# Cross attention over 25,088 context rows: six chunks mixed at a time in place of four, with V's projections and the splits of the context two chunks sooner

## The reference, cut to what matters

```
Q = LN(x) @ Wq + bq;  K = ctx @ Wk + bk;  V = ctx @ Wv + bv      # 16 heads of 32
scores = einsum('bihd,bjhd->bijh', Q, K) / sqrt(32)
attn = softmax(scores, axis=1)                                  # over the 256 queries i
out = einsum('bijh,bjhd->bihd', attn, V) @ Wo + bo
```

## Time and profile before

| | |
|---|---|
| median of 3 runs | 2655.68 us (2654.76 to 2655.82) |
| the profiled execution's own time | 2655.65 us |
| its span, first to last instruction | 2653.9 us |
| PE busy over the span | 2607.3 us (98%) |
| PE weight loads busy | 2203.0 us (83%) |
| DVE busy | 1968.5 us (74%) |
| ACT busy | 1866.0 us (70%) |
| POOL busy | 1272.1 us (48%) |
| mean granted TensorE clock | 0.993 of full speed |
| scores, first and last start | 511.9 and 2208.8 us |

### The profile page before, as it was taken

The page is one execution under the profiler, slowest core; times in us unless marked ns, Lnnn a source line. Parts: engine busy times, 40 slices in busy tenths (PEclk is TensorE's granted clock), DMA queues, the critical chain, the costliest instruction groups (busy, mean ns, idle before and its releaser), DMA issues.

```text
span 2653.9 us, 59616 instructions
## 1 busy us (share of the span) xinstructions
PE 2607.3 (98%) x21096; PEld 2203.0 (83%) x21096; DVE 1968.5 (74%) x3882; ACT 1866.0 (70%) x6834; POOL 1272.1 (48%) x2200
## 2 busy tenths in 40 slices
PE   8998999999999999999999999999999998999998
PEld 6876999888888888888888888888888885799997
DVE  8876866587778777778777778777787776655555
ACT  2213444388888888888888888888888895345553
POOL 5532111256566556566556665565665553222222
PEclk9998999999999999999999999999999999999999
DMA  9993553566666666666666666666666653545452
GB/s 385 387 399 116 193 195 151 135 171 182 159 158 163 165 167 159 165 159 158 174 166 159 158 165 161 167 161 167 158 155 175 166 126 110 192 175 190 182 191 72
DMA packets 132300, 473.33 MB, mean 178 GB/s; under 512 B 31128, under 2 KB 31256, under 8 KB 124832
## 3 DMA queue, kind: packets, MB, share of 16 engines
q1 hardware_dynamic: 122592, 452.21, 58.9%
q10 hardware_dynamic: 9408, 17.31, 1.7%
HBM read 244.47 MB, written 17.30 MB: 99 GB/s over the span
## 4 chain that ended last, share of the span: by engine, by line
PE 97%; DVE 2%; ACT 1%; issue 0%; DMA 0%; POOL 0%; SPq 0%; DVEq 0%; POOLq 0%
PE PB L592 21%; PE PB L619 15%; PE PB L627 14%; PE PB L607 14%; PE PB L695 7%; PE PB L418 7%; PE PB L710 6%; PE PB L554 6%; PE PB L567 3%; PE PB L447 1%; PE PB L478 1%; ACT EE L858 1%; PE PB L454 1%; PE PB L499 0%; DMA AR<-in_ctx 0%
## 5 line engine op out<-in xcount | busy, mean ns | idle before, releaser
L858 ACT ACTIVATE EE<-PB,small 128x256 f32<-128x256 f32 x3136 | 1445.0, 482 | 203.5 <-DVE small L1252 190.4
L1252 DVE TENSOR_REDUCE small<-PB 128x2 f32<-128x512 f32 x1568 | 1031.1, 682 | 355.5 <-PE PB L619 355.3
L858 ACT ACTIVATION_READ_ACCUMULATOR EE<-PB,small 128x1 f32 x3136 | 664.8, 212 | 0.0
L1514 POOL TENSOR_TENSOR VS<-V,small 128x128 f32<-128x128 f32 x784 | 320.5, 409 | 700.6 <-DVE small L1258 693.1
L592 PE MATMUL PB<-CTX,WKV 128*128 128x256 f32 x4704 | 624.9, 282 | 0.0
L592 PEld LDWEIGHTS PB<-CTX,WKV 128*128 128x128 f32 x4704 | 588.5, 190 | 0.1
L619 PEld LDWEIGHTS PB<-QS,STK 128*128 128x128 f32 x3136 | 469.5, 190 | 124.9 <-issue 82.3
L619 PE MATMUL PB<-QS,STK 128*128 128x256 f32 x3136 | 555.8, 289 | 7.5 <-ACT EE L858 5.4
L607 PE MATMUL PB<-WKV,CTX 128*128 128x512 f32 x1584 | 432.6, 395 | 0.8 <-DVE V L1248 0.8
L627 PE MATMUL PB<-EE,VS 128*32 128x256 f32 x6272 | 381.5, 384 | 0.0
L607 PEld LDWEIGHTS PB<-WKV,CTX 128*128 128x128 f32 x1584 | 273.1, 190 | 37.0 <-DVE V L1248 1.2
(11 more groups left out here) (202 smaller groups left out, 2545.8 us busy)
## 6 DMA issues: line engine op xcount, KB each, us to landing
STK<-KHL SPq DMA_DIRECT2D x1568, 128.0 KB, 2.5
RW<-in_l1f SPq DMA_DIRECT2D x32, 2048.0 KB, 8.0
AR<-in_ctx SPq DMA_DIRECT2D x49, 1024.0 KB, 8.5
RAW<-in_ctx SPq DMA_DIRECT2D x98, 512.0 KB, 3.7
WF<-in_l0f SPq DMA_DIRECT2D x17, 2304.0 KB, 8.8
v_scr<-RAW ACTq DMA_DIRECT2D x64, 256.0 KB, 7.5
V<-v_scr SPq DMA_DIRECT2D x64, 256.0 KB, 2.9
WA<-in_l0a SPq DMA_DIRECT2D x1, 4096.0 KB, 14.3
```

The lines of the kernel that those rows point to most:

```text
L858: m = e.activation(EE[:, b, s, :], bank(2 * (k % 2) + half, 256 * (s % 2), 256), ACT.Exp, bias=nm[:, b, s:s + 1], accum_out=su[:, b, s:s + 1])
L1252: e.tensor_reduce(nm[:, k % RING, 2 * half:2 * half + 2], bank(2 * (k % 2) + half).rearrange("p (s i) -> p s i", s=2), axis=AX.X, op=ALU.m ...
L1514: e.tensor_tensor(VS[:, b, :].rearrange("p (s d) -> p s d", s=4), V[:, t % 4, 128 * c:128 * c + 128].rearrange("p (s d) -> p s d", s=4), r ...
```

## The change

MIX goes from 4 to 6 and RING from 6 to 8. `due_v` is shifted by two chunks, so one more third of V's projection stands ahead of the loop. The high split's halves move from k % 8 = 2, 3 to 0, 1 and the low split's quarters from 3 to 6 to 1 to 4. EE grows by 8 KB in each partition; to make room OT and WO lie over places of KHL and STK that are no longer used near the end, so WO's load is issued behind the loop, when the scores of chunk 775 are done. The last mixing call takes the six chunks that no block has taken.

```diff
-MIX = 4
-RING = 6
+MIX = 6
+RING = 8
@@ def due_v(k):
-    n = (k + 14) // 6
-    return (n, (k + 14) % 6 // 2) if k % 2 and v_tile(n) < NT else None
+    n = (k + 16) // 6
+    return (n, (k + 16) % 6 // 2) if k % 2 and v_tile(n) < NT else None
@@ def build(nc, a):
         CTX = sb("CTX", [P, 3, 2, NC, GT], F32R, life)
+        late = ExitStack()
+        sb("khl_front", [P, 3, NC, GT], over=late)
+        OT = sb("OT", [P, NC, 256], over=late)
+        WO = sb("WO", [P, NC, D], over=late)
+        late.close()
...
-        EE = sb("EE", [P, RING, 4, 256], over=life)
-        OT = sb("OT", [P, NC, 256], over=life)
         q_life = ExitStack()
+        sb("ee_front", [P, 4, 4, 256], over=q_life)
         QHL = sb("QHL", [P, 2, NC, 256], F32R, q_life)
         q_life.close()
-        WO = sb("WO", [P, NC, D], over=life)
+        EE = sb("EE", [P, RING, 4, 256], over=life)
@@ def sync_program(e):
-                if k == 40:
-                    w.wait_ge("d_q", 256)
-                    e.dma_start(WO[:, :, :], a["l1x"][:, 2048:4096].rearrange("p (c n) -> p c n", c=NC)).then_inc(S["d_wo"], 16)
...
+            w.wait_ge("s_mm", 2 * (NCH - 8))
+            e.dma_start(WO[:, :, :], a["l1x"][:, 2048:4096].rearrange("p (c n) -> p c n", c=NC)).then_inc(S["d_wo"], 16)
@@ def tensor_program(e):
-            project_v(*due_v(-1))
+            for k in (-3, -1):
+                project_v(*due_v(k))
...
-            mix(NCH - 2)
-            mix(NCH - 1)
+            for n in range(NCH - NCH % MIX - 2, NCH):
+                mix(n)
@@ def vector_program(e):
-                if k % 8 in (2, 3) and k // 8 + 3 < NG:
+                if k % 8 in (0, 1) and k // 8 + 3 < NG:
                     split_hi(k // 8 + 3, (k % 2,))
@@ def gpsimd_program(e):
-                if 3 <= k % 8 <= 6 and k // 8 + 3 < NG:
-                    split_lo(k // 8 + 3, (k % 8 - 3,))
+                if 1 <= k % 8 <= 4 and k // 8 + 3 < NG:
+                    split_lo(k // 8 + 3, (k % 8 - 1,))
```

## The result

The changed kernel took 2708.1 us (median of four, 2707.66 to 2710.48), the kernel before, measured beside it, 2655.6 us: a ratio of 1.0204 with a 95% interval of 1.0192 to 1.0216. It is 2% slower; the forecast was 2705 us.

A forecast was written before the change was run, and what follows sets the result against it. PE was taken to set the pace, ACT having some slack. In 24 chunks, 2.24 us of stalls less 0.66 of saved switches lose 1.58, 31.5 times: 49.8 us, giving 2705 us from 2655.68; the forecast's own range is 2686 to 2716.

The forecast's parts named there:

- The fixed cost of a block: Switching PE to a block of mixing matmuls costs 0.33 us; 65 fewer blocks save 21.5 us, 0.66 in 24 chunks.
- The ordinary run: Three runs of six in four: V's add on chunk 1 delays chunk 2's exponentials; PE stalls 0.29 us at chunk 4.
- The run at a multiple of 24: Split halves on chunks 0 and 1 plus V's add make PE stall 0.24 us at chunk 3, 0.98 at chunk 4.
- ACT runs dry in a block.: During a mixing block no new scores come, so ACT sits idle (after 1553.9 until 1557.06) and must catch up.
- The run six chunks on: Run beginning at 6 mod 24: a split half at its chunk 2 adds 0.15 us to the 0.29 stall.
- The sum: In 24 chunks, stalls of 2.24 us less 0.66 saved lose 1.58; 31.5 times, 49.8 us.
- The released half's 0.11 us: Scores released by exponentials take 0.35 us for 0.24, weights loading late: 1.18 us from the exponentials' start instead of 1.07.
- The low split's move takes away a wait that the larger block would make: On GpSimd, unmoved quarters would delay the projection at k = 8 mod 24; moving them is worth nothing against before.
- Rival 1: ACT and DVE have enough slack, PE never waits, the saved switches come through: 2634 us, faster; chance 0.07.
- Rival 2: Only the collision of split, V's add and block costs, ordinary runs just fit: 18 us lost, 2673 us; chance 0.08.
- Rival 3: ACT is the bound, PE's saved time turns into equally long waits: 2655 us, within 0.2%; chance 0.03.
- rival 4: GpSimd or the low split is late too, a K projection waits 1.3 us in one run of four: 2746 us; chance 0.04.

The follow-up runs named there:

- the kernel with nothing shifted: Six chunks a block and eight places, V's projections and the splits where the kernel before had them; 2752.5 us, ratio 1.0370 to the kernel before.
- the last kernel: The best order with every third context group's splits one chunk sooner (high at 16 and 17 mod 24); 2635.5 us, ratio 0.9924 to the kernel before.
- both halves first: Changed kernel with both halves of scores ahead of the K or V projection in the first three chunks behind a block; 2652.9 us, ratio 0.9994 to before.
- the best order: Changed kernel with both score halves ahead of projections behind a block, V's projections as before, splits one chunk sooner than before; 2640.1 us, on a second turn 2645.7.
- V as before: Changed kernel with V's projections back where the kernel before had them (due_v with 14); 2686.6 us, ratio 1.0127 to the kernel before.

## Why the prediction was right

- **The fixed cost of a block, 0.33 us.** It measured 0.33 in the change's own block, and 0.64 us in 24 chunks once no stall covers it. The saving is real: 19.5 us for the kernel where nothing stalls (2654.9 against 2635.5), 21.5 forecast.
- **The ordinary run, 0.29 us of stall.** 12.86 us is the run with none; the change's runs at 18 and 12 mod 24 take 13.16 and 13.22: 0.30 and 0.36. In the latter the scores of the fifth chunk, the first chunk of a context group, start 1.16 us behind the exponentials in place of 1.07. That was not forecast, and its cause was not tried. The forecast's account of the 0.29 is incomplete: it follows DVE through V's add alone. With V's add moved away 0.27 us of the 0.30 stay, since ACT's own pace (chunk 1's exponentials at T+3.99, four at 0.45 us) ends only 0.05 us sooner. The size came out because the chain that was followed is the later of the two, and that by little.
- **The run at a multiple of 24, 0.24 + 0.98.** 14.07 - 12.86 = 1.21 us for 1.22. The price of the half behind V's add, 0.53, was right, but V's add is not what makes it: the last section shows GpSimd.
- **"ACT runs dry in a block."** This was misread. The bracket in the row says 0.34 us: before the change ACT was at work through the whole of that block and caught up there. In the changed kernel ACT is idle for 1.18 us ahead of its first exponentials of the run (chunk 480, at 1586.04). No term of the sum hangs on it.
- **The run six chunks on, 0.29 + 0.15.** 13.28 - 12.86 = 0.42 us for 0.44, of which the 0.29 holds as said above.
- **The sum.** 53.72 - 52.08 = 1.64 us lost in 24 chunks for 1.58. Between chunks 12 and 768 it is 51.6 us (2229.58 - 537.51 against 2180.75 - 540.23) for 49.8. Ahead of chunk 12 the changed execution was 2.7 us sooner, behind chunk 768 it took 3.8 us more. I had put both at nothing, and they nearly cancel by luck. The trace has 4.15 us more from chunk 768 to the last scores (32.20 for 28.05); why was not looked into.
- **The released half's 0.11 us.** At the low bound of 1.07 us the ordinary run would have stalled for 0.18; it does for 0.30, and 1.18 gives 0.29. The row read where PE had once waited was the right price.
- **Layout, eight places, WO's load: nothing.** Shown by the run with these alone.
- **The low split's move takes away a wait that the larger block would make.** This was right in kind, but the price was short. I had it wait in one run of four; the trace of the kernel with nothing shifted shows two, at chunks 488 and 496.
- **The rule that the most occupied engine is the one to relieve.** The Trainium skill (Perfetto Trace Analysis, Identifying the Most-Contended Engine) judges TensorE's headroom by the busy share of its weight loads (and by MFU, the share of peak arithmetic, not worked out here) beside the other engines' occupancy; by the weight loads ACT was ahead, and no gain would have come from fewer switches on PE. This case does not agree: the last kernel gains 19.5 us, and 0.64 us in 24 chunks is the price of two switches, with ACT at 352.72 us of 400. So for this stage PE's matmul time, with its waits beside it, was the better sign of the bound.

Rival 1 (the slack is enough) fell to the waits in the changed trace. Rival 2 (only the collision costs) fell with every ordinary run being at least 0.30 us longer than 12.86. Rival 3 fell with the result, and rival 4 with no wait of a K projection for GpSimd among the change's waits.

What the change ran into is therefore shown from three sides. Adding to DVE's list behind a block lengthens the kernel by nearly the same time. Moving V's add away from there gives 21 us back, nearly all of it in the run where the split halves collide with it. Feeding DVE and ACT sooner from PE gives back all but that collision, the ordinary stall included, which neither V's add nor the split halves explain by themselves.

## What to carry to other kernels

An engine that sets the pace can be held up by one with plenty of idle time, if the idle time lies in one place and the debt in another. Before a batch is made larger, lay down the start times of one full period by hand, for every supplier: ACT's own row, which the working left out, came within 0.05 us of DVE's. A pause on the bounding engine (here the block) is where its suppliers do their other work; a larger batch makes the pauses rarer, and that other work, moved by a few steps for the sake of another wait, then lands in the catching-up. Feed the starved engines first behind a pause: the order of two instruction groups on the bounding engine cost nothing and turned 2% lost into level; with V's add and the split halves moved as well, it became 0.8% won.

## What the hardware showed that I had not expected

- The time of a DVE copy from SBUF to SBUF in FP32 (a split half) depends on what GpSimd is at as it begins. With GpSimd at nothing it takes 0.39 us (56 copies of the change's trace between 600 and 2100 us) or, behind K's copy, 0.42 (29 copies with both halves first). Where GpSimd is at an operation in SBUF as the copy begins, all 112 copies of the change's trace end 0.28 us behind that one: a copy takes 0.47 beside the scaling of V (84 copies) and 0.76 beside K's subtraction in the best order (1588.67 + 0.74 = 1589.41 against 1588.93 + 0.76 = 1589.69). The 0.60 of the half behind V's add is this too, and not V's add: GpSimd was at K's high part, and 1590.23 + 0.40 = 1590.63 against 1590.31 + 0.60 = 1590.91.

```profile
1590.23 0.40 POOL L1528 CAST KHL<-KR 128x256 fp32r<-128x256 f32 x1
```

The Trainium skill (SBUF — State Buffer, section SBUF: two separate sides) says that such a copy and a GpSimd operation lock each other out of a shared pair of ports for a whole instruction; these traces agree.
- A wait on a matmul whose semaphore comes in time for the matmul but not for the load of its weights still costs about 0.1 us, and shows at most as an idle time of PEld. With V as before, 23 halves of scores between chunks 12 and 760 start on time, 0.12 us behind the matmul ahead of them, and yet have the next instruction 0.34 us behind them in place of 0.24. In the change's trace PEld's waits for ACT are 60.8 us, beside 29.7 us under PE: who reads PE's row alone misses most of the places where the time went.
